# Two row pairs of each attention batch turned through device memory, and one score group moved

## What is computed

```
Q = x @ W_q;  K = x @ W_k;  V = x @ W_v
scores = einsum('bqe,bke->bqk', Q, K) / sqrt(512)
out = einsum('bqk,bke->bqe', softmax(scores), V) @ W_o
x = x + out
x = x + ffn(layernorm(x))
```

## Time and profile before

| what | value |
|---|---|
| median of 3 runs | 933.51 us (932.82 to 933.73) |
| the profiled execution | 933.69 us, of which the traced span is 931.9 us |
| PE busy | 918.5 us, 99% of the span |
| DVE, ACT, POOL busy | 630.9, 444.3, 429.5 us |
| batch 0 of phase B | about 485 to 608 us of the span |
| batch 1 of phase B | about 608 to 717 us |

### The profile page before, as it was taken

One profiled execution on the slowest core, in us unless ns is written; L12 is line 12 of the kernel. 1 busy time (PEld: TensorE's weight loads), 2 busy tenths in 40 slices (PEclk: granted clock), 3 DMA queues, 4 the chain that ended last, 5 costly groups with the idle time before them and its releaser, 6 DMA issues.

```text
span 931.9 us, 13051 instructions
## 1 busy us (share of the span) xinstructions
PE 918.5 (99%) x4534; PEld 513.7 (55%) x4550; DVE 630.9 (68%) x1171; ACT 444.3 (48%) x884; POOL 429.5 (46%) x448
## 2 busy tenths in 40 slices
PE   7999999999999999999999999999999999999998
PEld 4888888888743444444444444444444444444444
DVE  6555666848777687777754878547776777765643
ACT  4433334356567723664343445324444685346620
POOL 5442424466547645665640143420515566546530
PEclk9999999999999999999999999999999999999999
DMA  9401300024031172003812728215471002910001
GB/s 318 181 13 34 135 15 34 1 80 148 13 124 46 24 120 39 2 0 57 125 46 46 113 46 153 52 23 95 65 113 24 1 1 34 192 46 1 1 34 57
DMA packets 239952, 61.75 MB, mean 66 GB/s; under 512 B 226768, under 2 KB 227088, under 8 KB 239504
## 3 DMA queue, kind: packets, MB, share of 16 engines
q1 hardware_dynamic: 239888, 60.92, 29.2%
HBM read 41.47 MB, written 19.43 MB: 65 GB/s over the span
## 4 chain that ended last, share of the span: by engine, by line
PE 87%; DVE 5%; POOL 2%; SPq 2%; issue 2%; ACT 1%; DMA 1%; DVEq 0%; POOLq 0%
PE psum L2327 49%; PE psum L2574 14%; PE psum L2576 13%; PE psum L2724 8%; PE psum L2376 1%; PE psum L2365 1%; SPq L801 1%; SPq L820 1%; PE psum L2461 1%; DVE ln_bn L1620 1%; DVE wv_lo L1711 1%; DMA xres<-x 1%; DVE s_f L2155 0%; DMA turned<-blocks 0%; POOL hid L1034 0%
## 5 line engine op out<-in xcount | busy, mean ns | idle before, releaser
L1038 POOL TENSOR_TENSOR hid<-hid,hid_hi 128x512 f32<-128x512 f32 x88 | 102.9, 1169 | 104.1 <-DVE hid_hi L1976 104.1
L2574 PE MATMUL psum<-xf,w_gu 128*128 128x512 f16 x352 | 133.9, 380 | 0.7 <-DVE yt L2058 0.7
L2574 PE MATMUL psum<-xf,w_s 128*128 128x512 f16 x264 | 100.1, 379 | 1.5 <-DVE up L1949 1.3
L2576 PE MATMUL psum<-xf,w_gu 128*128 128x512 f16 x264 | 100.1, 379 | 0.0
L2327 PE MATMUL psum<-wd_low,hid_lo 128*128 128x512 bf16 (+1 forms) x330 | 73.8, 373 | 0.2
L1361 ACT ACTIVATE hid_lo<-hid 128x512 f16<-128x512 f32 x88 | 54.9, 624 | 33.1 <-POOL hid L1038 33.1
L1034 POOL TENSOR_TENSOR hid<-up,gate 128x512 f32<-128x512 f32 x44 | 56.0, 1272 | 25.2 <-ACT gate L1356 25.2
L2576 PE MATMUL psum<-xq,w_s 128*128 128x512 f16 x176 | 66.7, 379 | 0.0
L2574 PEld LDWEIGHTS psum<-xf,w_gu 128*128 128x128 f16 x352 | 34.3, 97 | 55.4 <-ACT acc L1346 15.5
L1356 ACT ACTIVATE gate<-gate,sg_xs 128x512 f32<-128x512 f32 x44 | 31.7, 721 | 58.6 <-DVE gate L1959 58.6
L2327 PEld LDWEIGHTS psum<-wd_low,hid_lo 128*128 128x128 f16 x330 | 32.2, 98 | 36.9
(11 more groups left out here) (354 smaller groups left out, 2414.9 us busy)
## 6 DMA issues: line engine op xcount, KB each, us to landing
prob_blocks<-probs SPq DMA_DIRECT2D x60, 128.0 KB, 2.8
back<-prob_blocks SPq DMA_DIRECT2D x40, 128.0 KB, 3.0
turned<-blocks SPq DMA_DIRECT2D x36, 128.0 KB, 3.2
cla_wide<-cla_dram SPq DMA_DIRECT2D x16, 256.0 KB, 3.3
out<-xres SPq DMA_DIRECT2D x15, 256.0 KB, 2.0
xres<-x SPq DMA_DIRECT2D x3, 1024.0 KB, 13.0
blocks<-xn SPq DMA_DIRECT2D x24, 128.0 KB, 3.0
codes_gu<-gateT SPq DMA_DIRECT2D x1, 2816.0 KB, 11.6
```

The costliest lines, as they stand in the source:

```text
L1038: nc.gpsimd.tensor_tensor(hid[:, :], hid[:, :], hid_part(hid_hi, j, half), ALU.subtract).then_inc(rest_done, 1)
L2574: nc.tensor.matmul(bank(use[0]), w, x_operand(piece, k, False), start=start and k == 0, stop=False, skip_group_check=not start)
L2576: last = nc.tensor.matmul(bank(use[0]), w, x_operand(piece, k, True), start=False, stop=k == 1, skip_group_check=not start)
```

## The change

For pairs 0 and 1 of sets B1 and F2, `turn_both` and `x_copy` are dropped. VectorE transposes `xn` in 32x32 blocks in place (`pair_turned`, a 128x1024 transpose), SyncE sends it out (`pair_to_dram`, four transfers of 128 KB) and fetches it into a widened `x_first` (`pair_to_slot`, four more); ScalarE and VectorE read the pair from there and not from PSUM. As `xn` is shared, `x_normalise` of pairs 1 and 2 waits until the pair before is out. Pair 1's fetch stands ahead of tile 4's `probs_to_dram` in SyncE's order; it waits until pair 0's parts are made. For room, `x_last` of place 2 lies over `sd_rows`, which is fetched again in batch 1. The bank use counts are lowered to suit.

TensorE's order also changes: `first_row(3)`, the scores of row tile 6 and part of 7, moves from before `attend(3)` to between its halves. On VectorE `x_normalise(q, 0)` and `x_normalise(q, 1)` move ahead, and the four `x_stats` that stood together before `query_parts` are spread over the row groups behind it. `x_rstd` of rows 4 to 7 moves behind pair 0's parts on GpSimd.

```diff
@@ transfers @@
-                    for b in range(BATCHES):
-                        for i in range(BT - b):
-                            probs_turned(b, i)
-                            if (b, i) == (0, IN_PLACE):
-                                weights_back(1)
+                    for b, s in enumerate((B1, F2)):
...
+                        if b == 1:
+                            down_scales()
+                        probs_to_dram(b, 2)
+                        pair_to_dram(s, 0)
+                        probs_back(b, 2)
+                        probs_to_dram(b, 3)
+                        pair_to_slot(s, 0)
+                        probs_back(b, 3)
+                        pair_to_dram(s, 1)
+                        pair_to_slot(s, 1)
+                        probs_to_dram(b, 4)
+                        probs_back(b, 4)
...
+            def pair_to_dram(q, i):
+
+                sp.wait_ge(pair_blocks_done, sent_n(q, i) + 1)
+                src = xn[:, :].rearrange("p (m j) -> p m j", j=SQ)
+                for a in range(QUADS):
+                    sp.dma_start(pair_blocks[sent_n(q, i), a].rearrange("m (c i) j -> i (m c) j", c=QUADS),
+                                 src[a * SQ:(a + 1) * SQ, :, :]).then_inc(pair_out, 16)
+
+            def pair_to_slot(q, i):
+
+                n = 4 * q + i
+                sp.wait_ge(pair_out, sent_all(q, i))
+                if i > 0:
+                    sp.wait_ge(x_ab_lo, n)
+                    sp.wait_ge(x_t34_done, 2 * n)
+                    sp.wait_ge(pair_2_lo, sent_n(q, i))
+                elif q == F2:
+                    job = q_job(1, 1, 3)
+                    Use(sp, "B", 1).full((job % 2, job // 2))
...
@@ ScalarE @@
-                x_both(0)
+                x_row_highs(q, 0)
...
-                x_both(1)
+                x_row_highs(q, 1)
                 pT_high(4)
                 softmax(6)
                 x_12_high(q, 1)
+                pT_high(5)
                 x_34_high(q, 1)
                 part_sum(7, 3)
-                pT_high(5)
...
@@ VectorE @@
+            def pair_turned(q, i):
+                dve.wait_ge(ln_xn_done, ln_n("X", q, 2 * i + 1) + 1)
+                nc.vector.transpose(xn[:, :], xn[:, :]).then_inc(pair_blocks_done, 1)
+
             def x_normalise(q, i):
+                if q in (B1, F2) and 0 < i <= SENT:
+                    dve.wait_ge(pair_out, sent_all(q, i - 1))
...
+                x_normalise(q, 0)
                 p_blocks(2)
+                pair_turned(q, 0)
...
-                x_normalise(q, 0)
                 p_blocks(3)
-                for l in range(4, 8):
-                    x_stats(q, l)
+                x_normalise(q, 1)
                 query_parts(b, 1, 0)
                 pT_low(2)
                 query_parts(b, 1, 1)
+                pair_turned(q, 1)
                 out_add(1)
...
@@ TensorE @@
                 attend(1)
-                turn_both(0)
                 first_row(2)
                 attend(2, 0, 4)
                 score(7, 2)
                 attend(2, 4, 8)
                 score(4, 2)
-                turn_both(1)
+                attend(3, 0, 4)
                 first_row(3)
-                attend(3)
+                attend(3, 4, 8)
                 attend(4, 0, 4)
```

More of the change, by code:

```diff
@@ L866, in probs_turned, with down_scales @@
                                  prob_blocks[n, a].rearrange("m p j -> p m j")).then_inc(p_moved[i % 2], 16)
+            def pair_to_dram(q, i):
[14 more added lines that the diff above has]
+                    Use(sp, "B", 1).full((job % 2, job // 2))
+                dst = pair_slot(q)[:, :].rearrange("p (m a j) -> p m a j", a=QUADS, j=SQ)
+                for a in range(QUADS):
+                    sp.dma_start(dst[:, :, a, :],
+                                 pair_blocks[sent_n(q, i), a].rearrange("m p j -> p m j")).then_inc(pair_back, 16)
+            def down_scales():
+                sp.dma_start(sd_rows[:, :], s_down.partition_broadcast(P)).then_inc(sd_in, 16)
             weights_out()
@@ L1113, in pairs_of @@
                     x_12_low(q, i)
+                    if i == 0:
+                        x_rstd(q, *range(4, 8))
             def weight_sums(*which):
@@ L1122, in _ @@
             query_parts(0, 1)
-            x_rstd(B1, *range(4, 8))
             pairs_of(B1)
@@ L1129, in _ @@
             query_parts(1, 1)
-            x_rstd(F2, *range(4, 8))
             pairs_of(F2)
@@ L1659, in x_second @@
                     Use(dve, phase, b).read_out(one)
-                    t, first, done = bank(two[0]), x_first[v][:, :], drained[two[0]]
+                    t, first, done = bank(two[0]), x_first_of(q, i), drained[two[0]]
                 dve.wait_ge(x_b2_hi, n + 1)
@@ L2278, in _ @@
                 row_max(4)
[L2279 removed]
+                x_stats(q, 5)
                 p_blocks(4)
                 x_34_low(q, 0)
+                x_stats(q, 6)
                 pT_low(3)
```

70 lines of the change are left out of this document (54 added, 16 removed).

## The result

The changed kernel takes 937.96 us in the median of four runs (937.25 to 938.75), the one before 933.16 us (931.60 to 933.73) beside it. The ratio is 1.0055, with a 95% interval of 1.0042 to 1.0067: slower by about 5 us. The forecast was 936.1, with a range of 933.2 to 939.3. It stood on a median of 933.51 us and 2.6 us more; against the kernel measured beside it the change cost 4.8.

What follows compares the result with a forecast made beforehand. The prediction took TensorE, busy 99% of the span, as the bound. Removing 4.46 us and adding 7.04 us of waits gave net +2.58 us on 933.51, so 936.1 us, range 933.2 to 939.3.

Steps and rivals of the forecast that it cites:

- What is removed: TensorE's work and wait for turning pairs 0 and 1: 2.23 us less a batch, 4.46 in all.
- Part 1: Wait before piece 6 of first_row(2) for the second low query part: 0.3 us a batch, 0.6 in all.
- Part 2: Wait before attend(3) for pT_low(3), behind row tile 6's statistics: 0.94 us a batch, 1.88 in all.
- Part 3: Wait before attend(4) for pT_low(4), with half of attend(3) in between: 1.88 us a batch, 3.76 in all.
- Part 4: End of the batch: waits of 0.3 us before attend(6) in batch 0 and 0.5 before turn_last in batch 1.
- The rule weighed: VectorE instructions with two SBUF inputs slow beside GpSimd: x_second(0) some 1.4 us later, sum 1 us higher; left out.
- A: Rival: faster, as TensorE never waits for pT_low(3) and pT_low(4); 929.7 us, chance 0.07.
- B: Rival: in the stage, removed work and added waits nearly cancel; 933.4 to 934.7 us, chance 0.23.
- C: Rival: SyncE's transfers collide, one bundle's delay of 2.3 us in each batch; 940.7 us, chance 0.10.

Runs made afterwards that it cites:

- e11: e7 with ScalarE's high part of tile 2 behind the second query's a_highs and VectorE's low part behind the second query_parts; 930.67 us, ratio 0.9976.
- e6: The changed kernel with VectorE's statistics of row tile 6 behind pT_low(3) and not ahead of it; 935.58 us, ratio 1.0032.
- e4: The changed kernel with VectorE's x_normalise(3) ahead of x_second(2) and not behind out_add(4); 935.87 us, ratio 1.0039.
- e5: e1 with VectorE's x_normalise(3) ahead of x_second(2), as in e4; 931.00 us, ratio 0.9984.
- e8: The changed kernel with both VectorE edits, x_normalise(3) earlier (e4) and the statistics of row tile 6 later (e6); 933.17 us, ratio 1.0008.
- e10: The changed kernel with pair 1's fetch issued behind tile 4's send and not ahead of it; 937.06 us, ratio 1.0043.
- e9: e7 with pair 1's fetch issued behind tile 4's send and not ahead of it; 932.40 us, ratio 0.9995.
- e1: The changed kernel without the split: attend(3) undivided behind first_row(3), pairs still sent through memory; 933.37 us, ratio 1.0015.
- e7: e5 with score(4, 2) between the third and fourth quarter of attend(2) and not behind all of it; 930.52 us, ratio 0.9984.
- e12: e11 with one eighth of attend(3) between the second and third piece of first_row(3), the rest behind it; 930.16 us, ratio 0.9980.
- e3: The changed kernel with VectorE's pT_low(4) ahead of the last additions and the maximum of row tile 6; 940.22 us, ratio 1.0090.

## Why the prediction was right or wrong

The time lay in the range and on the forecast's side of no change. The likeliest time, 936.1, was 1.9 us short of the median. On the traced execution the forecast was 936.3 against 937.25; another 0.7 us are between the traced execution and the median of its kernel, and no trace shows them. The direction was no luck, as all the waits stand where they were named. The size is weaker than the hit in the range makes it look: 2.6 us more were forecast, and measured were 3.8 on the stage and 4.8 on the medians.

**What is removed** was right: with the waits subtracted, the stage is 2.21 us shorter in each batch, where 2.23 were forecast.

**Part 1**, 0.6 us forecast, 0.58 + 0.05 = 0.63 measured. The size was right, one reason wrong. The second `s_lo` came 0.25 us earlier against `attend(1)`, not 0.75. `x_normalise(1)` did end 1.2 us earlier than the statistics before it, but behind the first query part the high part of tile 2 holds ScalarE, and tile 2's fetch, now behind pair 0's send, ended its issue 1.1 us later against `attend(1)`. The prediction had written that this fetch "loses little". e11 shows it.

**Part 2**, 1.88 forecast, 0.85 + 0.84 = 1.69 measured, and e6 shows its cause: the row that was named and no other.

**Part 3**, 3.76 forecast, 1.79 + 1.79 = 3.58 measured. The chain of 4.32 us held to 0.01: `first_row(3)` ended at 563.26 and `pT_low(4)` at 566.37 + 1.22 = 567.59. What was too large, here and in part 2, is the 0.15 us from semaphore to matmul, for which the prediction names no row; `attend(4)` started 0.05 us behind `pT_low(4)`, and `attend(3)` 0.06 behind `pT_low(3)`. The two rows of VectorE, its first addition and this one:

```profile
563.46 0.69 DVE L2273 TENSOR_TENSOR probs<-psum,probs 128x512 f32<-128x512 f32 x1
...
566.37 1.22 DVE L2296 SCALAR_TENSOR_TENSOR even_lo<-back,even_hi 128x1024 f16<-128x1024 f32 x1
```

**Part 4** is the step that failed: 0.3 and 0.5 forecast, 1.65 and 0.67 measured, so 2.32 for 0.8, and the bound of 1 for batch 0 was passed. Behind the start of `attend(1)`, `pT_low(6)` ended 1.7 us later than forecast in batch 0, and two things make this up.

The larger is the length of VectorE's chain. I wrote that VectorE runs "the same instructions without a real gap, 8.4 us". It doesn't run them in the same order. The diff moves `out_add(4)` ahead of `x_normalise(3)`, and I didn't price that move. In the kernel before, the two normalising instructions ran beside GpSimd's two instructions of `x_sums`, of which the second is shown:

```profile
576.28 1.44 DVE L1630 TENSOR_SCALAR xn<-xres,xmv,xrstd 128x512 f32<-128x512 f32 x2
```

```profile
576.53 0.91 POOL L912 TENSOR_TENSOR x_last<-x_first,x_mid 128x256 f32<-128x256 f32 x1
```

Behind `out_add(4)`, 1.1 us later in VectorE's order, they run beside `x_ab_low` and `x_12_low` and take 2.57 us. From the start of `pT_low(5)` to the end of `pT_low(6)` are 8.41 us before and 9.50 in the changed kernel, 1.1 us more.

The smaller is the start of that chain. `pT_low(5)` was to start 40.5 us behind the start of `attend(1)` (575.3 less 534.77) and started 41.1 behind it. It stands behind the high part of tile 5, for which ScalarE waited on the fetch:

```profile
572.19 1.06 ACT L1579 ACTIVATE xb_hi<-back 128x1024 f16<-128x1024 f32 x1 [1.67 <-DMA back<-prob_blocks]
```

e4 and e5 show that the wait goes when GpSimd no longer slows the two instructions. They take off 1.57 us where the move had added 1.13, so they show more than the cost of the move; no run restores the old order alone. In batch 1 the two took 1.70 us before and 1.83 after, so the move cost almost nothing there, and the 0.67 us before `turn_last` are close to the 0.5 forecast.

The waits come to 8.2 us where 7.04 were forecast, and 8.2 - 4.46 = 3.8 is the stage's growth.

**The rule weighed** did not act where I looked for it. `x_second(0)` ended on time and VectorE was not slowed. Its last instruction, with two SBUF inputs, took 0.68 us, and GpSimd's beside it 1.11 us, where the same takes 0.73 at 576.53:

```profile
543.82 0.68 DVE L1755 TENSOR_TENSOR xb_lo<-x_first,xb_hi 128x512 f16<-128x512 f32 x1
```

```profile
543.98 1.11 POOL L980 TENSOR_TENSOR x_last<-x_mid,x_first 128x256 f32<-128x256 f32 x1 [2.36 <-DVE x_mid L1753]
```

What GpSimd slowed was the one-input instruction that I had not thought of, since I had read the section for its first half only. About the 1 us that I set beside the sum by this rule came, but from another line, which is luck.

**The rivals.** A fell, at the point named for it: `pT_low(4)` doesn't end within 2.4 us of `first_row(3)`. B needed parts 1, 2 and 4 small; e8 comes near that, at 933.2 us. C did not happen in its size in the changed kernel, though a fetch did hold a high part, by the 1.67 us of part 4; e10 shows that the fetch's place didn't matter there, and e9 that it does once the waits in front are gone.

**What was missed beyond the steps** is in e1. `turn_both(1)` hid the emptying of a bank, and 0.7 us behind that comes the next wait, for tile 4's buffer (e7). In the changed kernel the first half of `attend(3)` covers both, so the sum didn't suffer; but by the same steps the sending alone would have been forecast 4.46 - 0.6 - 0.8 = 3.1 us faster, and its stage is 0.2 us shorter.

## What to carry to other kernels

On an engine that is 99% busy, every piece of work is also the cover of what lies behind it: before one is taken out, list for the next operands, banks and buffers how long ahead of their turn they are ready. Price every line of a diff that changes places on another engine, also where the set of instructions stays the same; a move of 1 us can put an instruction beside other work of GpSimd, as here, where 1.44 us became 2.57, and with GpSimd idle 1.00. Splitting a product to fill a gap pays only as far as the part left behind is as long as the chain that it hid: here an eighth split off cost 0.07 us before the next product and a half cost 1.8 us. And what is won in front has to outlast the transfers: in e8 and e12 a gain of 0.7 to 0.8 us in batch 0 came back as a wait for a fetch.

## What the runs showed of the hardware

Two normalising instructions of 128x512 in 32 bits, one SBUF input each, took 1.00 us alone and 2.57 us beside GpSimd, and a `pT_low` of 128x1024 took 2.17 us and not 1.21 (e3). The loser isn't always VectorE: beside `x_second(0)` it was GpSimd's instruction that stretched, from 0.73 to 1.11 us. In these three pairs the one that was stretched had started second: VectorE's at 578.07 behind 577.90 and at 574.50 behind 573.98, GpSimd's at 543.98 behind 543.82.

TensorE fell to the lower clock with no single idle time longer than 2.5 us, after stretches of 5 us in which it had worked for 2.66 and 2.96 us (e7, e3), and lost 1.7 us by it each time. In the changed kernel, with single waits of 1.8 us between full stretches, the granted clock stayed at 1.0.

The stage's transfers kept their engines busy for 0.57 and 0.58 of the time, against 0.46 and 0.43 before; these are the table's rows for the two batches in the changed kernel (us; busy time and instructions of each engine; clock; transfer share; GB/s):

```profile
485.00:608.50 123.50, 119.29 (x559) 54.30 (x557) 87.88 (x146) 51.00 (x81) 38.22 (x38) 1.00 0.57 94
608.50:717.00 108.50, 105.75 (x501) 48.70 (x498) 79.72 (x136) 46.55 (x74) 34.89 (x33) 1.00 0.58 90
```

The issue of four transfers then took up to 3.92 us (pair 0's send, at 523.83), where the earlier trace rows have 2.27 and 2.51; the longest of the kernel before in the two batches is 3.49, at 684.43.
